# Expert results scattered to token order job by job, and the closing sums shared by VectorE, TensorE and ScalarE

## The chip, the cores and the metric

One core of one Trainium2 chip runs the whole program. The metric is the device time of one execution in microseconds (us), the median over timed runs. A core has TensorE (PE in the profile), VectorE (DVE), ScalarE (ACT), GpSimd (POOL) and SyncE (SP). In this kernel SP and POOL issue all DMAs, each on a queue of its own; the transfers are carried out by the same 16 DMA engines.

## The reference, cut to what matters

```python
x = L0_attn_x                                    # (8, 512, 256) float32
x = _layernorm(x + _L0_attn_ref(x, ...))         # state-space recurrence over 512 steps
x = _layernorm(x + _L0_ffn_ref(x, ...))
x = _layernorm(x + _L1_attn_ref(x, ...))
x = _layernorm(x + _L1_ffn_ref(x, gate_w, fc_w, proj_w))

def _L1_ffn_ref(x, gate_w, fc_w, proj_w):        # E = 8 experts, K = 2 chosen of them
    gates = softmax(xt @ gate_w)                 # 4096 tokens of 256 numbers
    top_v, top_i = top_k(gates, 2);  top_v = top_v / sum(top_v)
    h = gelu(einsum('nd,edf->enf', xt, fc_w))    # 256 -> 1024
    eo = einsum('enf,efd->end', h, proj_w)       # 1024 -> 256
    out = sum over the two chosen experts of top_v * eo
```

The change lies in the last line of the program: the mixture of experts, the sum of a token with its two weighted expert results, and the last layer norm.

## The kernel before, in words

Three phases follow each other. `project_phase` (0 to 296 us) makes the inputs of the recurrence. `stream_phase` (to about 4650 us) runs the recurrence, 2048 updates by GpSimd (L1611) and VectorE (L1649), beside the dense layers, and writes the finished tokens to the DRAM tensor `mixed`. In its half-steps `k`, SP's loop `body` loads `decay` (dt_rows, L713; ScalarE's exponential L1263 waits for it), rows for TensorE, weights, and in every second half-step one piece of 64 rows of a filler into the DRAM tensor `slots` (L799), 512 pieces in all, so that no row of it is ever undefined.

`expert_phase` computes only the chosen experts. Tokens are handled in 8 sequences `s` (groups) of 4 tiles of 128.

- Choosing: for each group TensorE turns x (`turned_x`, L2070) and computes the logits, VectorE picks the two experts (`choose`) and the row in `slots` of each choice (`index`: 4096 rows per expert). GpSimd scatters every tile twice to its rows (L2019, 64 indirect DMAs of 128 rows of 1 KB).
- Jobs: up to `RUN` = 39 jobs, each 256 rows of one expert. For job `j` GpSimd gathers the expert's weights (`fetch(j)`, L1998 and L2002, 1 MB each, double buffered) and the rows of job `j + 2` (`tokens`, L2010, ring `xs` of 4). TensorE's order is turn(j), down(j-1), up(j). ScalarE does the gelu, VectorE copies the result into `made[j % 2]` (`result`, L2341), and SP stores it row by row of the job to `expert_out` (`store`, L1979).
- Close: when the last store has landed, SP raises `all_out`, and GpSimd gathers for each of 32 tiles its two result rows by `slot` (L2036, 64 indirect DMAs of 128 rows of 1 KB into `got`). For each group VectorE adds both results, weighted by `share` (L2356, L2360), takes the statistics (L2364, L2367), waits for ScalarE's 1/sqrt(variance) (Ln L2184, Exp L2186) and normalises (L2371); SP stores the group (L1987).

The order on POOL's queue is written by hand:

```python
            for j in range(2, RUN):
                fetch(j)
                if j + 2 >= XS and j + 2 < RUN:
                    tokens(j + 2)
            pool.wait_ge(slot_ok, 1)
            pool.wait_ge(all_out, 1)
            for c in range(TILES):
                for k in range(2):
                    pool.indirect_dma_start(got[:, k, c], None, d["EXPERT_OUT"], ...
```

## Time and profile before

| | |
|---|---|
| timed runs, median of 3 | 5430.61 us (5424.06 to 5439.41) |
| profiled execution, span of all instructions | 5453.5 us |
| PE / DVE / ACT / POOL busy, share of the span | 86% / 71% / 62% / 73% |
| stretch of the recurrence, 296 to 4320 us | 4024 us |
| stretch of the jobs, 4772 to 5352 us | 580 us |
| from there to the end | 101 us |

For the profiled execution the page gives the span (first to last instruction) and no time measured as in the timed runs; its span lies 22.9 us (0.4%) above their median. Sums below are made inside the span and then applied to the median. A stage is to be read by itself: the engines' shares of the whole span mix a recurrence, a stretch of matmuls and a closing stretch.

### The profile page before, as it was taken

To read this page: it belongs to the slowest core of one execution; us is meant where nothing else is said; L and a number is where in the kernel's file an instruction comes from. 1 tells how busy PE (TensorE), PEld (TensorE's weight loads), DVE (VectorE), ACT (ScalarE), POOL (GpSimd) and SP (SyncE) were. 2 spreads that over 40 slices of the span, in tenths; PEclk is the share of its full clock that TensorE was granted. 3 is DMA by queue.
4 is the path that set the end of the run, shared out by engine and by line. 5 is a ranking of instruction groups with operands and counts; after the bars stand their busy time and mean duration, and the time that the engine had idled before them with its cause. 6 is when DMAs were issued, how large, how long until landed. Compare 5 with 4: busy or idle time off the path is not lost. (4 is left out here: it accounts for less than half of the span.)

```text
span 5453.5 us, 69165 instructions
## 1 busy us (share of the span) xinstructions
PE 4700.0 (86%) x21182; PEld 1804.0 (33%) x21182; DVE 3887.2 (71%) x4378; ACT 3382.7 (62%) x3973; POOL 3994.4 (73%) x2350
## 2 busy tenths in 40 slices
PE   8569999998999899889989998899889887399992
PEld 4301112223223222222222222223222343388882
DVE  6868888888988898789889987988798621400003
ACT  6646666778777877777777777777867633011112
POOL 0079998998999899889989998899899700522224
PEclk9855558989999899899989998999899898599996
DMA  3367676776777677767767776677677521345553
GB/s 114 124 220 256 244 241 236 271 258 236 254 263 261 229 256 254 255 228 256 262 242 252 255 267 236 242 262 263 224 252 262 195 66 43 134 166 175 181 175 113
DMA packets 319255, 1189.13 MB, mean 218 GB/s; under 512 B 77424, under 2 KB 116976, under 8 KB 308912
## 3 DMA queue, kind: packets, MB, share of 16 engines
q1 hardware_dynamic: 296624, 1071.70, 55.8%
q0 software_dynamic: 22272, 113.00, 6.2%
q8 instruction: 182, 2.98, 0.2%
q14 instruction: 177, 1.45, 0.1%
HBM read 1129.21 MB, written 88.87 MB: 223 GB/s over the span
## 5 line engine op out<-in xcount | busy, mean ns | idle before, releaser
L1611 POOL TENSOR_TENSOR s_h<-s_decay,s_h 128x768 f32<-128x768 f32 x2048 | 3705.8, 1849 | 306.4 <-ACT s_decay L1263 283.8
L1649 DVE TENSOR_TENSOR s_h<-s_h,bank 128x1024 f32<-128x1024 f32 x2048 | 2469.8, 1215 | 394.6 <-POOL s_h L1611 210.9
L1263 ACT ACTIVATE s_decay<-s_decay,s_a_neg 128x1536 f32<-128x1536 f32 x1024 | 1606.4, 1569 | 204.1 <-DMA s_decay<-dt_rows 202.8
L895 PE MATMUL bank<-s_h,s_cdiag 128*32 128x512 f32 x8192 | 1259.5, 691 | 10.1 <-ACT s_y L1275 10.1
L1268 ACT ACTIVATE bank<-bank,s_a_neg 128x512 f32<-128x512 f32 x1024 | 672.5, 657 | 678.5 <-PE bank L883 676.0
L869 PE MATMUL bank<-s_vrow,s_brow 9*128 9x512 bf16 x4096 | 847.8, 423 | 277.5 <-DVE s_h L1649 248.5
L869 PEld LDWEIGHTS bank<-s_vrow,s_brow 9*128 9x128 bf16 x4096 | 209.1, 92 | 1504.9 <-issue 1501.6
L1639 DVE TENSOR_TENSOR s_h<-bank,s_h 128x512 f32<-128x512 f32 x1024 | 698.7, 682 | 2.3 <-ACT bank L1268 1.3
L1007 PE MATMUL bank<-m_mb,m_w 128*128 128x512 f32 x1024 | 519.9, 637 | 1.9 <-ACT m_u L1406 1.1
L993 PE MATMUL bank<-m_ma,m_w 128*128 128x512 f32 x1024 | 517.3, 634 | 0.0
L883 PE MATMUL bank<-s_drow,s_unit 3*128 3x512 bf16 x1024 | 433.1, 423 | 76.0 <-DMA s_drow<-dt_parts 46.9
L2172 ACT ACTIVATE e_hid<-bank 128x512 f32<-128x512 f32 x156 | 93.0, 597 | 462.8 <-PE bank L2048 462.8
L895 PEld LDWEIGHTS bank<-s_h,s_cdiag 128*32 128x32 f32 x8192 | 169.7, 114 | 404.5 <-issue 387.0
L2048 PE MATMUL bank<-e_pj,e_hid 128*128 128x256 f32 x1248 | 278.6, 381 | 12.0 <-issue 12.0
L2048 PE MATMUL bank<-e_cT,e_fc 128*128 128x256 f32 x1248 | 277.5, 381 | 0.8 <-DVE e_cT L2336 0.8
L883 PEld LDWEIGHTS bank<-s_drow,s_unit 3*128 3x128 bf16 x1024 | 96.4, 94 | 492.6 <-issue 469.0
L2048 PEld LDWEIGHTS bank<-e_pj,e_hid 128*128 128x128 f32 x1248 | 233.9, 190 | 50.5 <-issue 20.3
L2048 PEld LDWEIGHTS bank<-e_cT,e_fc 128*128 128x128 f32 x1248 | 238.2, 191 | 33.9 <-issue 1.2
L1007 PEld LDWEIGHTS bank<-m_mb,m_w 128*128 128x128 f32 x1024 | 181.6, 195 | 199.9 <-issue 197.7
L993 PEld LDWEIGHTS bank<-m_ma,m_w 128*128 128x128 f32 x1024 | 181.2, 194 | 200.3 <-issue 200.2
L1992 POOL MEMSET e_eps<- 128x1 f32 x1 | 0.1, 99 | 327.2 <-POOLq L2410 327.2
L2336 DVE COPY e_cT<-bank 128x256 f32<-128x256 f32 x39 | 16.6, 425 | 300.4 <-PE bank L2108 300.4
(220 smaller groups left out, 4035.4 us busy)
## 6 DMA issues: line engine op xcount, KB each, us to landing
s_decay<-dt_rows SPq DMA_DIRECT2D x1024, 768.0 KB, 5.4
m_w<-in_units SPq DMA_DIRECT2D x210, 512.0 KB, 5.2
s_vrow<-v_parts SPq DMA_DIRECT2D x1024, 36.0 KB
slots<-in_x_tiles SPq DMA_DIRECT2D x512, 64.0 KB, 4.3
s_brow<-b_parts SPq DMA_DIRECT2D x1024, 9.0 KB
v_parts<-p_part SPq DMA_DIRECT2D x24, 512.0 KB, 3.0
expert_out<-e_made SPq DMA_DIRECT2D x39, 256.0 KB, 6.2
m_w<-w_scaled SPq DMA_DIRECT2D x16, 512.0 KB, 3.7
```

Of the source, the lines that this page charges most:

```text
L869: mm = pe.matmul(bank[:, X0 + n % 2 * PAIR + b], brow[q:q + PAIRS, buf, hf, at * STATE:(at + 1) * STATE], vrow[q:q + PAIRS, buf, hf, at * ...
L883: pe.matmul(bank[:, E0 + hf], unit[q:q + PARTS], drow[q:q + PARTS, buf, t % STEPS], start=True, stop=True).then_inc(e_ps, 1)
L895: mm = pe.matmul(bank[q * 32:(q + 1) * 32, Y0], cdiag[:, hf * LANES + q, at * BLK:(at + 1) * BLK], h[:, t % 2, hf * LANES + q], start=(at ...
L993: mm = pe.matmul(bank[:, j % 4 if tail else M0], w[:, slot, k * P:(k + 1) * P], ma[:, k], start=(k == 0), stop=(k == KH - 1))
L1007: mm = pe.matmul(bank[:, j % 4 if tail else M0], w[:, slot, k * P:(k + 1) * P], mb[:, k], start=(k == 0), stop=(k == KH - 1))
L1263: act.activation(decay[:, k % RING], decay[:, k % RING], ACT.Exp, scale=a_neg[:, 1:2]).then_inc(decay_ok, 1)
L1268: act.activation(bank[:, E0 + k % HALVES], bank[:, E0 + k % HALVES], ACT.Exp, scale=a_neg[:, 1:2]).then_inc(e_ok, 1)
L1611: pool.tensor_tensor(h[:, t % 2, g * PAIR:(g + 1) * PAIR, DCOLS:], decay[:, k % RING, g % 2 * PAIR:(g % 2 + 1) * PAIR], h[:, (t + 1) % 2, ...
L1639: dve.tensor_tensor(h[:, t % 2, hf * LANES:(hf + 1) * LANES, 0:DCOLS], bank[:, E0 + hf].rearrange("p (b d) -> p b d", b=LANES), h[:, (t + ...
L1649: dve.tensor_tensor(h[:, t % 2, g * PAIR:(g + 1) * PAIR], h[:, t % 2, g * PAIR:(g + 1) * PAIR], bank[:, X0 + n % 2 * PAIR:X0 + (n % 2 + 1) ...
L2048: mm = pe.matmul(dst, lhs(k), rhs(k), start=(k == 0), stop=(k == n - 1))
L2172: act.activation(hid[:, r, 2 * m:2 * m + 2].rearrange("p m t -> p (m t)"), bank[:, m], ACT.Gelu).then_inc(up_ok, 1)
```

## The change

Three pieces.

- **Home rows.** A token's row in `slots` grows from 256 to 258 numbers: the two extra ones are `home` (2 × its token number, loaded once) and its second choice (`owner`, VectorE). Job `j` computes on VectorE, from the rows it has gathered, where each result belongs in token order (`goals`: 2 × token, + 1 if the job's expert is the token's second choice; rows that belong to no token go to a dump area). The filler's rows have 258 numbers too.
- **Scatter by job.** GpSimd scatters each job's results to `expert_out` in token order (`give(j - 2)` behind `fetch(j)` and `tokens(j + 2)`, the last three behind the loop). SP's stores and the 64 gathers are gone; at the end SP loads each group's results with one plain DMA of 1 MB (`load`, a ring of `GOT` = 4 buffers).
- **Close.** Of each group's 4 tiles VectorE sums two and TensorE two (identity times x plus two diagonal matrices `weigh` times the results, made by ScalarE in every second job); VectorE takes the statistics of all four and the product `shift` = -mean × rstd; ScalarE normalises (4 activations), into x; SP stores. ScalarE's table for Ln and Exp is set once.

Core of the diff:

```diff
@@ stream_phase, body
-                        sp.dma_start(d["SLOTS_FILL"][(c * HALF_STEPS + k) // FILL_EVERY], d["x_rows"]
+                        sp.dma_start(d["SLOTS_FILL"][(c * HALF_STEPS + k) // FILL_EVERY], d["fill"]
@@ expert_phase
+ROW = DIM + 2
+SUMMED = (0, 1)
+OTHERS = (2, 3)
+GOT = 4
-        x = sb("e_x", [P, TILES, DIM])
-        got = sb("e_got", [P, 2, TILES, DIM])
+        x = sb("e_x", [P, TILES, ROW])
+        got = sb("e_got", [P, GOT, TT, 2, DIM])
+        weigh = sb("e_weigh", [P, BATCH * len(SUMMED), 2, P])
-        xs = sb("e_xs", [P, XS, JT, DIM])
+        xs = sb("e_xs", [P, XS, JT, ROW])
@@ SP
-            for j in range(RUN):
-                store(j, j % 2)
-            sp.wait_ge(made_out, 16 * (RUN + 1))
-            sp.sem_inc(all_out, 1)
+            def load(s):
+                sp.dma_start(got[:, s % GOT], d["EXPERT_OUT_TILES"][s]).then_inc(got_in[s], 16)
+            for r in range(2):
+                sp.wait_ge(made_out[r], 16 * JT * ((RUN + 1 - r) // 2))
+            for s in range(GOT):
+                load(s)
             for s in range(BATCH):
                 sp.wait_ge(y_ok, (s + 1) * TT)
-                sp.dma_start(out[s], got[:, 0, s * TT:(s + 1) * TT]).then_inc(out_dma, 16)
+                if s + GOT < BATCH:
+                    load(s + GOT)
+                sp.dma_start(out[s], x[:, s * TT:(s + 1) * TT, 0:DIM]).then_inc(out_dma, 16)
@@ GpSimd
                 if j >= XS:
                     pool.wait_ge(T_ps, LEAD + j - XS + 1)
+                    pool.wait_ge(goal_ok, j - XS + 1)
+            def give(j):
+                pool.wait_ge(goal_ok, j + 1)
+                pool.wait_ge(made_ok, LEAD + j + 1)
+                for i in range(JT):
+                    pool.indirect_dma_start(d["EXPERT_OUT"], bass.IndirectOffsetOnAxis(ap=goal[:, i, j:j + 1], axis=0),
+                                            made[:, j % 2, i], None).then_inc(made_out[j % 2], 16)
             for s in range(BATCH):
                 pool.wait_ge(x_in[s], 16)
+                pool.wait_ge(home_ok, 1)
+                pool.wait_ge(owner_ok, s + 1)
                 pool.wait_ge(in_ok, s + 1)
@@
-            pool.wait_ge(slot_ok, 1)
-            pool.wait_ge(all_out, 1)
-            for c in range(TILES):
...
+                give(j - 2)
+            for j in (RUN - 2, RUN - 1):
+                give(j)
@@ TensorE
+            def sums(s):
+                n = len(SUMMED)
+                pe.wait_ge(weigh_ok, (s + 1) * 2 * n)
+                if s >= GOT:
+                    pe.wait_ge(y_ok, (s - GOT + 1) * TT)
+                pe.wait_ge(got_in[s], 16)
+                for q, i in enumerate(SUMMED):
+                    dst = bank[:, s % GOT * len(SUMMED) + q, 0:DIM]
+                    pe.matmul(dst, w["ident"][:], x[:, s * TT + i, 0:DIM], start=True, stop=False)
+                    for k in range(2):
+                        mm = pe.matmul(dst, weigh[:, s * n + q, k], got[:, s % GOT, i, k], start=False, stop=(k == 1))
+                    mm.then_inc(sum_ps, 1)
@@ ScalarE
+                if j % 2 == 0 and j // 2 <= BATCH * len(SUMMED):
+                    weights(j // 2 - 1)
             act.wait_ge(eps_ok, 1)
+            act.preload_act_table_set("natural_log_exp_and_others")
...
+                act.wait_ge(ln_ok, s + 1)
+                act.wait_ge(shift_ok, s + 1)
+                for i in range(TT):
+                    c = s * TT + i
+                    whole = bank[:, s % GOT * len(SUMMED) + SUMMED.index(i), 0:DIM] if i in SUMMED else x[:, c, 0:DIM]
+                    act.activation(x[:, c, 0:DIM], whole, ACT.Identity, bias=shift[:, c:c + 1],
+                                   scale=rstd[:, c:c + 1]).then_inc(y_ok, 1)
@@ VectorE
+            def goals(j):
+                dve.wait_ge(xs_in[j % XS], 16 * JT * (j // XS + 1))
+                dve.scalar_tensor_tensor(out=aim[:, :, j], in0=xs[:, j % XS, :, DIM + 1], scalar=whose[:, j:j + 1],
+                                         in1=xs[:, j % XS, :, DIM], op0=ALU.is_equal, op1=ALU.add).then_inc(aim_ok, 1)
...
             def result(j, r):
-                dve.wait_ge(made_free, LEAD + j)
+                if j >= 2:
+                    dve.wait_ge(made_out[r], 16 * JT * (j // 2))
...
+            for s in range(BATCH + 1):
+                if s < BATCH:
+                    dve.wait_ge(got_in[s], 16)
+                    for i in OTHERS:
+                        add(0, s, i)
+                if s:
+                    shifts(s - 1)
+                if s < BATCH:
+                    for i in OTHERS:
+                        add(1, s, i)
+                    statistics(s)
```

How the change moves instructions, at three places (the rows give line, operation, names out<-in and shape; `x2` is a count).

**GpSimd, the end of its queue.** Before, `e_xs` are the gathered tokens, `e_fc` and `e_pj` a job's weights, `e_got` the results gathered at the end:

```order
L2010 DMA e_xs<-slots,e_source 128x256 x2
L1998 DMA e_fc<-in_fc,e_rows 128x2048
L2002 DMA e_pj<-in_pj,e_rows 128x2048
L1998 DMA e_fc<-in_fc,e_rows 128x2048
L2002 DMA e_pj<-in_pj,e_rows 128x2048
L2036 DMA e_got<-expert_out,e_slot 128x256 x64
L1889 UNCONDITIONAL_BRANCH
```

and now, where L2028 is `give` and its last six are the results of jobs 36, 37 and 38:

```order
L2019 DMA e_xs<-slots,e_source 128x258 x2
L2028 DMA expert_out<-e_made,e_goal 18433x256 x2
L2006 DMA e_fc<-in_fc,e_rows 128x2048
L2010 DMA e_pj<-in_pj,e_rows 128x2048
L2028 DMA expert_out<-e_made,e_goal 18433x256 x2
L2006 DMA e_fc<-in_fc,e_rows 128x2048
L2010 DMA e_pj<-in_pj,e_rows 128x2048
L2028 DMA expert_out<-e_made,e_goal 18433x256 x6
L1894 UNCONDITIONAL_BRANCH
```

The 64 gathers are gone from behind the last job; two scatters stand in each job, and two behind the last result.

**SyncE, the expert phase.** Before:

```order
L1968 DMA e_pcol<-in_pcol 128x1
L1970 DMA e_x<-mixed 128x1024 x8
L1973 DMA e_made<-in_pcol 128x1
L1979 DMA expert_out<-e_made 128x2x256 x39
L1987 DMA out<-e_got 128x1024 x8
L1889 UNCONDITIONAL_BRANCH
```

and now, where `e_home` and `e_dump` are two new small tables, and x is written and read in rows of 256 numbers because its rows have 258:

```order
L1979 DMA e_home<-in_home 128x32
L1979 DMA e_dump<-in_dump 128x80
L1981 DMA e_x<-mixed 128x4x256 x8
L1985 DMA e_got<-expert_out 128x2048 x5
L1995 DMA out<-e_x 512x1x256
L1985 DMA e_got<-expert_out 128x2048
L1995 DMA out<-e_x 512x1x256
L1985 DMA e_got<-expert_out 128x2048
L1995 DMA out<-e_x 512x1x256
L1985 DMA e_got<-expert_out 128x2048
L1995 DMA out<-e_x 512x1x256 x5
```

The 39 stores are gone; loads of groups 4 to 7 stand each ahead of a group's store.

**VectorE, one group of the close.** Before, `e_st` and `e_mv` are statistics, the last row is the normalisation:

```order
L2356 SCALAR_TENSOR_TENSOR e_x<-e_got,e_share,e_x 128x256 x4
L2360 SCALAR_TENSOR_TENSOR e_x<-e_got,e_share,e_x 128x256 x4
L2364 BN_STATS e_st<-e_x 128x6 x4
L2367 BN_AGGR e_mv<-e_st 128x2 x4
L2371 TENSOR_SCALAR e_got<-e_x,e_mv,e_rstd 128x256 x4
```

and now, with the previous group's `e_shift` between the two additions:

```order
L2427 SCALAR_TENSOR_TENSOR e_x<-e_got,e_share,e_x 128x256 x2
L2447 SCALAR_TENSOR_TENSOR e_shift<-e_mv,e_rstd 128x4
L2427 SCALAR_TENSOR_TENSOR e_x<-e_got,e_share,e_x 128x256 x2
L2434 BN_STATS e_st<-e_x 128x6 x2
L2437 BN_STATS e_st<-bank 128x6 x2
L2440 BN_AGGR e_mv<-e_st 128x2 x4
```

Half of the additions and the whole normalisation have left VectorE; the statistics of two tiles are read from TensorE's `bank`.

## Rows read from the trace of the kernel before

**Rows 1.** busy time by stage: us, PE, PEld, DVE, ACT, POOL busy (instructions), granted clock, DMA share, GB/s

```profile
296.00:4320.00 4024.00, 3644.82 (x16935) 1036.74 (x16936) 3463.11 (x3546) 2951.25 (x3338) 3703.04 (x2046) 0.89 0.71 251
...
4772.00:5352.00 580.00, 567.09 (x2651) 491.65 (x2652) 42.84 (x77) 105.14 (x196) 137.50 (x145) 1.00 0.51 168
...
5368.00:5454.00 86.00, 0.00 (x0) 0.00 (x0) 50.23 (x160) 24.55 (x32) 56.01 (x55) 0.50 0.42 134
```

**Rows 2.** the end in order of time (start us, us): last job, first and last group

```profile
5352.68 0.69 DVE L2341 COPY e_made<-bank 128x512 f32<-128x512 f32 x1 [14.09 <-PE bank L2048]
5356.42 0.95 POOL L2036 DMA_INDIRECT e_got<-expert_out,e_slot  x1 [32.20 <-SPq L1984]
...
5368.07 1.67 DVE L2356 SCALAR_TENSOR_TENSOR e_x<-e_got,e_share,e_x 128x256 f32<-128x256 f32 x4 [14.70 <-DMA e_got<-expert_out,e_slot]
...
5369.66 1.67 DVE L2360 SCALAR_TENSOR_TENSOR e_x<-e_got,e_share,e_x 128x256 f32<-128x256 f32 x4
...
5371.25 1.40 DVE L2364 BATCH_NORM_STATS2 e_st<-e_x 128x6 f32<-128x256 f32 x4
...
5372.56 0.36 DVE L2367 BATCH_NORM_AGGREGATE e_mv<-e_st 128x2 f32<-128x6 f32 x4
...
5374.61 1.28 ACT L2186 ACT_TABLE_LOAD   x1
...
5376.22 1.38 DVE L2371 TENSOR_SCALAR e_got<-e_x,e_mv,e_rstd 128x256 f32<-128x256 f32 x4 [3.29 <-ACT e_rstd L2186]
...
5439.52 0.95 POOL L2036 DMA_INDIRECT e_got<-expert_out,e_slot  x1 [0.30 <-issue]
5442.24 1.67 DVE L2356 SCALAR_TENSOR_TENSOR e_x<-e_got,e_share,e_x 128x256 f32<-128x256 f32 x4 [1.35 <-DMA e_got<-expert_out,e_slot]
```

**Rows 3.** one job in order of time, all engines

```profile
5079.10 0.38 ACT L2166 ACTIVATE e_cT<-bank 128x256 f32<-128x256 f32 x1
...
5086.28 7.07 PE L2048 MATMUL bank<-e_cT,e_fc 128*128 128x256 f32 x32
...
5086.72 0.95 POOL L2002 DMA_INDIRECT e_pj<-in_pj,e_rows  x1 [6.93 <-PE bank L2048]
...
5089.23 0.96 POOL L2010 DMA_INDIRECT e_xs<-slots,e_source  x1 [0.30 <-issue]
...
5093.63 0.95 POOL L1998 DMA_INDIRECT e_fc<-in_fc,e_rows  x1 [3.43 <-PE bank L2048]
```

**Rows 4.** DMA of the expert stage (4770 to 5353 us): KB each, median us to landing

```profile
expert_out<-e_made SPq DMA_DIRECT2D x38, 256.0 KB, 6.2
```

**Rows 5.** DMA issues of 1 KB rows and of whole groups: KB each, median us to landing

```profile
out<-e_got SPq DMA_DIRECT2D x8, 512.0 KB, 3.0
...
v_parts<-p_part SPq DMA_DIRECT2D x24, 512.0 KB, 3.0
```

**Rows 6.** busy time in a stretch whose DMA engines are full (columns as in Rows 1)

```profile
4759.00:4771.00 12.00, 0.00 (x0) 0.00 (x0) 0.00 (x0) 0.00 (x0) 9.26 (x10) 0.50 0.96 372
```

**Rows 7.** the tile e_fc: duration of its matmuls, ns min/median/max

```profile
L2048 PE MATMUL bank<-e_cT,e_fc x1248: 379/379/763, 4774.0 to 5344.3; 128*128 128x256 f32 x179
```

**Rows 8.** start of the expert phase in order of time

```profile
4657.25 0.43 SPq L1968 DMA_DIRECT2D e_pcol<-in_pcol  x1
4657.73 4.32 SPq L1970 DMA_DIRECT2D e_x<-mixed  x8
...
4661.36 3.75 PE L2070 MATMUL bank<-e_ident,e_x 128*128 128x128 f32 x16 [18.10 <-DMA e_x<-mixed]
...
4675.89 1.07 POOL L2019 DMA_INDIRECT slots<-e_x,e_slot_in  x1 [21.27 <-DVE e_slot_in L2241]
```

**Rows 9.** the tensor slots: duration of the issuing instruction, ns min/median/max, first and last start

```profile
L799 SPq DMA_DIRECT2D slots<-in_x_tiles x512: 495/556/2302, 319.2 to 4314.1; - x171
...
L2019 POOL DMA_INDIRECT slots<-e_x,e_slot_in x64: 965/969/1075, 4675.9 to 4756.2; - x64
```

**Rows 10.** who waited for whom in the recurrence (296 to 4320 us): us, times, longest

```profile
ACT s_decay L1263 <- DMA s_decay<-dt_rows: 202.8, 149, 12.4
```

More of the change, by code:

```diff
@@ L1929, in expert_phase @@
         slotf = sb("e_slotf", [P, 2, TILES])
-        slot = sb("e_slot", [P, 2, TILES], U32)
         whose = sb("e_whose", [P, JOBS])
@@ L1935, in expert_phase @@
         rstd = sb("e_rstd", [P, TILES])
+        shift = sb("e_shift", [P, TILES])
         eps = sb("e_eps", [P, 1])
@@ L2143, in _ @@
             down(RUN - 1, (RUN - 1) % 2, (RUN - 1) // 2)
+            def sums(s):
[10 more added lines that the diff above has]
+                    mm.then_inc(sum_ps, 1)
+            for s in range(BATCH):
+                sums(s)
         @block.scalar
@@ L2173, in gelu, with weights @@
                                    ).then_inc(up_ok, 1)
+            def weights(n):
+                c = n // len(SUMMED) * TT + SUMMED[n % len(SUMMED)]
+                for k in range(2):
+                    act.activation(weigh[:, n, k], w["ident"][:], ACT.Copy, scale=share[:, 2 + k, c:c + 1]
+                                   ).then_inc(weigh_ok, 1)
             turned(0)
             gelu(0, 0)
+            act.wait_ge(share_ok, 4)
             for j in range(1, RUN):
@@ L2252, in _ @@
                     choose(s - 1)
+                    owner(s - 1)
                 if s >= 2:
@@ new lines, in add, with statistics @@
+            def add(k, s, i):
+                c, n = s * TT + i, s * (TT - len(SUMMED)) + OTHERS.index(i) + 1
+                if k:
+                    dve.wait_ge(sum1, n)
+                dve.scalar_tensor_tensor(out=x[:, c, 0:DIM], in0=got[:, s % GOT, i, k], scalar=share[:, 2 + k, c:c + 1],
+                                         in1=x[:, c, 0:DIM], op0=ALU.mult, op1=ALU.add).then_inc(sum2 if k else sum1, 1)
+            def statistics(s):
+                for i in OTHERS:
+                    dve.wait_ge(sum2, s * len(OTHERS) + OTHERS.index(i) + 1)
+                    dve.bn_stats(st[:, s * TT + i], x[:, s * TT + i, 0:DIM]).then_inc(st_ok, 1)
+                for q, i in enumerate(SUMMED):
+                    dve.wait_ge(sum_ps, s * len(SUMMED) + q + 1)
+                    dve.bn_stats(st[:, s * TT + i], bank[:, s % GOT * len(SUMMED) + q, 0:DIM]).then_inc(st_ok, 1)
+                for n, i in enumerate(OTHERS + SUMMED):
+                    dve.wait_ge(st_ok, s * TT + n + 1)
+                    dve.bn_aggr(mv[:, s * TT + i], st[:, s * TT + i]).then_inc(mv_ok, 1)
@@ new lines, in shifts @@
+            def shifts(s):
+                tiles = slice(s * TT, (s + 1) * TT)
+                dve.wait_ge(ln_ok, s + 1)
+                dve.wait_ge(mv_ok, (s + 1) * TT)
+                dve.scalar_tensor_tensor(out=shift[:, tiles], in0=mv[:, tiles, 0], scalar=-1.0, in1=rstd[:, tiles],
+                                         op0=ALU.mult, op1=ALU.mult).then_inc(shift_ok, 1)
+            dve.wait_ge(share_ok, 4)
+            for s in range(BATCH + 1):
[6 more added lines that the diff above has]
+                if s < BATCH:
+                    for i in OTHERS:
+                        add(1, s, i)
+                    statistics(s)
```

113 lines of the change are left out of this document (49 added, 64 removed).

## The prediction

> **What bounds the kernel now.** I read the stages first, because the shares over the whole span mix them. In the recurrence GpSimd is busy 3703 of 4024 us; in the stretch of the jobs TensorE is busy 567 of 580 us at the full clock (2.4 GHz); in the last 86 us TensorE does nothing, and neither VectorE (50 us) nor ScalarE (25 us) nor the DMA engines (42%) is full [rows 1]. A stage in which nothing is full is bound by an order. The timeline of the end shows which one. The last result is copied from 5352.68 us; the first gather starts at 5356.42 and the 64th at 5439.52, so 63 of them take 83.1 us, 1.32 us each; the first group's sums start at 5368.07, the last group's at 5442.24, 2.7 us behind the last gather [rows 2], and 11.3 us on, of which 3.0 are the last store [rows 5], the span ends at 5453.5 us. The close is bound by GpSimd writing one indirect DMA after another, and after each eighth VectorE has its group long before the next. The change is aimed at the 101 us behind the last matmul, so its gain cannot exceed that.
>
> **The close, new.** Step by step, on the clock of the profiled execution:
>
> - Copy of the last result ends at 5353.4. Two scatters are issued by GpSimd, the second from 5353.5 + 1.26 = 5354.8 (1.26 us is the pitch between the start of e_pj and of the second e_xs, 2.51 us for two [rows 3]). An indirect transfer of the same size landed 2.7 us after its start (5439.52 to 5442.24 [rows 2]). So the results lie in DRAM at 5357.5. Upper bound: 6.2 us to landing, as SP's stores take when they queue beside weights [rows 4]; I take 2.7, since no weights are in flight any more.
> - First load. The first x group, 0.52 MB, was used 3.6 us after its issue [rows 8]. Full DMA engines moved 372 GB/s [rows 6], so another 0.52 MB is 1.4 us: 1.05 MB arrives after 5.0 us, at 5362.5. Before, the first group could start at 5368.1.
> - VectorE per group. Additions start 0.40 us apart (four in 1.59, from 5368.07 to 5369.66), statistics 0.33 (four in 1.31), the four aggregations 0.36 [rows 2]. Four additions, four statistics, the aggregations and one shift on 4 numbers a lane (no row; between 0.1 and 0.2 us, as one of the four aggregations at 0.09 and a gap) give 1.59 + 1.31 + 0.36 + 0.2 = 3.5 us. It was 6.3 us of work plus a wait of 3.3 us for ScalarE, in which two table loads of 1.28 us lay [rows 2]; those loads are gone, and the wait is filled with the next group's first additions.
> - TensorE: 6 matmuls per group. Their pace is 7.07 us for 32 = 0.22 us at the full clock [rows 3]; at the clock of 0.50 that the close shows now [rows 1] (1.2 GHz) a matmul takes twice as long (379 against 763 ns at most [rows 7]): 2.7 us per group, below 3.5.
> - ScalarE: Ln and Exp, about 0.7 us without the table loads (3.29 less 2 x 1.28), then 4 activations of 0.38 us at most [rows 3]: 2.3 us per group, below 3.5.
> - DMA: 8.4 MB in and 4.2 MB out are 12.6 MB, at 372 GB/s 33.8 us, 4.2 us per group. That is more than VectorE's 3.5, but the first four loads need not wait for a store. The eighth load has 10.0 MB ahead of it and in it, 26.8 us, behind the 2.2 us of the first load that are not its bytes (3.6 - 1.4): 5357.5 + 2.2 + 26.8 = 5386.5. VectorE would want it at 5362.5 + 7 x 3.5 = 5387.0. The two are level.
> - The end: 5387.0 + 3.5 + 0.7 + 0.2 + 1.4 (four activations, overlapped) = 5392.8, plus 3.0 for the store = 5395.8. Stores now go out of x in rows of 1 KB. The transfer v_parts has such rows and the same 512 KB, and took 3.0 us, like the old store of 4 KB rows [rows 5].
>
> The close is shorter by 5453.5 - 5395.8 = 57.7 us. I take 2 us off for handovers in the eight groups, which is a choice.
>
> "DMA: Bandwidth & Descriptors" of the Trainium skill, section "Where 436 GB/s comes from", says that between HBM and SBUF the HBM side binds at about 358 GB/s for a core. The row has 372 with 4% of the engines' time idle, so the trace does not agree, and it decides; by the page 12.6 MB would take 35.1 us, an estimate, and the sum would be 1.3 us worse.
>
> **The start of the expert phase.** Two more small loads stand ahead of x on SP, 0.47 us each (4657.25 to 4657.73 [rows 8]): 0.95 us. Loads of x in 1 KB rows: 0, by the same v_parts row, up to 0.5. Two `owner` instructions stand ahead of the first slot index on VectorE, 0.1 to 0.2 us each: 0.3. Everything behind is tied to the first scatter at 4675.89 [rows 8] by 64 scatters back to back, 0.97 us each [rows 9] and 1.27 apart, over 81 us; VectorE's 6 new and 6 removed small instructions on job tables hide under them. Together +1.5 us. I take the price of a scatter unchanged at 1032 bytes a row, because e_pj, 8 KB a row, is issued in 0.95 us and a row of 1 KB in 0.96 [rows 3]: the number of rows sets it.
>
> **The jobs.** GpSimd's queue gets two scatters per job, 2.51 us. Today it issues e_pj and two e_xs from 5086.72 to 5090.2 and waits until 5093.63 for TensorE, 3.4 us [rows 3]; 2.5 fit into that, and even late weights would have over a job's length before TensorE needs them, since fetch(j) asks for what up(j) uses one and a half jobs on. `give(j - 2)` waits for a copy that VectorE has done when e_pj is issued, so nothing is held behind it. VectorE may overwrite `made[j % 2]` only when the scatter has landed: issued 5 us behind down(j-2), landed by 6.2 us more at the worst [rows 4], wanted two jobs (29.6 us) behind. VectorE's three tiny goal instructions and ScalarE's two diagonals lie under 7 us of matmuls. DMA is 51% busy there [rows 1], and the bytes are the same. Price 0; if the cover were gone, 39 jobs times what sticks out.
>
> **The recurrence.** The filler moves 64 x 1032 bytes instead of 64 x 1024, 512 times, 0.8% more of 33.5 MB. Of 1010 MB in that stage (251 GB/s for 4024 us [rows 1]) the filler is 3.3%, so 95 us of the DMA engines' busy 2857 us. 0.8% of that is below 1 us. I take 0. Below it nothing is to be had; above, pieces of 4128 bytes no longer start on round addresses, for which there is no row. ScalarE already waits 202.8 us in 149 places for decay rows [rows 10] that queue behind the filler on SP, so what the filler loses counts at those places.
>
> On this the same page of the Trainium skill, section "How a descriptor splits into AXI transactions", says that a piece not starting at a multiple of 256 bytes also pays for the bytes in front of it. By it 4128 bytes would cost at most 6% more than 4096, an estimate: 6 us of engine time spread over the recurrence, 1 to 6 us on the sum if it all showed. No row of this case shows it.
>
> **The sum.** -57.7 + 2 + 1.5 + 0 + 0 = -54 us: 5453.5 becomes 5399 in the span. On the median of the runs, 22.9 us below the span, 5430.6 becomes **5377 us**, 1.0% less.
>
> **The rivals.**
>
> 1. *The close is paced by transfers, not by VectorE.* It now reads and writes at once, and half of its transfers have rows of 1 KB. If stores only reach the 175 GB/s of v_parts taken alone (524 KB in 3.0 us [rows 5]) and loads 372, the bytes take 22.6 + 24 = 46.5 us instead of 33.8: +13, 5390 us. For it: 4.2 against 3.5 us per group is already no margin. Against: the 3.0 us contain a fixed part.
> 2. *The scatters of 1032-byte rows are dearer to issue.* If each row becomes two pieces and the price doubles, 64 x 0.97 = 62 us come back ahead of the first job: 5439 us. It decides from 0.84 us more per scatter. Against: 8 KB and 1 KB rows cost the same.
> 3. *The filler slows the recurrence; the kernel gets slower.* If the odd pieces double its 95 us of engine time and all of it falls on the 149 waits of ScalarE, GpSimd's chain grows by 95 us: 5377 + 95 = 5472 us. It decides from 54 us on the path. For it: DMA is 71% busy there and decay rows do arrive late. Against: 149 of 1024 loads are waited for at all, so a share of the added time, not the whole, would show.
> 4. *GpSimd's longer queue holds up the jobs.* 6 issues of 1.26 us are 7.5 of a job's 14.8 us, so it would take a wait that I have not seen; 1 us per job is 39 us: 5416 us.
>
> **How the numbers follow.** Forecast 0.74, rival 1 0.13, rival 2 0.04, rival 3 in full 0.03, rival 4 0.03, others 0.03. The predicted time is the forecast's. Its own range: downward the handovers and the start may cost nothing (3.5 us), the first load may come 1 us earlier, and two medians of runs that lie 6.5 us under and 8.8 over it may differ by 10 more: 5362. Upward the filler may cost 6, the landing of the last scatter 3.5 and the runs' spread 8.8: 5395. With rival 1, the filler and the spread the upper end is 5405; what is left out is under 2 in 10. 0.3% of this kernel, 16 us, is about what a measurement can tell from no change. Faster by more: forecast, rival 1 and part of the others, 0.91. Within: rivals 2 and 4, 0.05. Slower: rival 3 and what is unforeseen, 0.04.
>
> **What would show it.** Right: the first group's additions start some 6 us earlier after the last matmul than now; groups follow each other at 3.5 to 4.5 us on VectorE; from the last matmul to the end 43 to 46 us instead of 101; jobs still 14.8 us apart and e_fc issued at the same moment after up(j-2); scatters still 1.27 us apart; the recurrence within 5 us of 4024 and ScalarE's wait for decay near 203 us. Wrong: groups at over 5 us with VectorE waiting for e_got (rival 1), a scatter over 1.1 us (2), a wait for decay that has grown by tens of us (3), a TensorE that waits for weights (4).

## The result and the profile after

The change is faster: 5388.73 us median of 4 runs (5380.9 to 5396.29) against 5429.31 us of 4 runs of the kernel before, ratio 0.9917 [0.9899, 0.9935]. That is 40.6 us, with an interval of 35 to 55 us; forecast were 54 us and a time of 5377 in a range from 5362 to 5405. The profiled execution has a span of 5387.5 us. One run of this study (of a_combo, 5703.85 us) went at a granted TensorE clock of 0.766 in place of 0.88 to 0.89 and stands in no ratio or median.

Most of the spread between executions comes from the recurrence: over the 14 profiles of this study it takes 3974 to 4010 us from the first to the last update of `s_h` on GpSimd, and kernels with and without the change lie mixed in that range. So I judge by a stretch that does not contain it. From the load of `e_gate` to the end (the expert phase) it is 4654.51 to 5453.5 = 799.0 us before and 4636.26 to 5387.5 = 751.2 us after: **47.8 us less**. Its parts (here and below such stretches are differences of starts, good to 0.1 us):

| stretch | forecast | before | after | difference |
|---|---|---|---|---|
| `e_gate` load to first scatter (start) | +1.5 | 21.4 | 26.3 | +4.9 |
| first scatter to first `turn` | 0 | 96.2 | 96.4 | +0.2 |
| from there to the copy of the last result | 0 | 580.6 | 581.5 | +0.9 |
| copy of the last result to the end (close) | -57.7 + 2 | 100.8 | 47.0 | -53.8 |

The stages of the kernel after (columns as in [rows 1]); the third row is the close, which answers to the last of [rows 1]:

```profile
296.00:4302.00 4006.00, 3634.43 (x16942) 1035.00 (x16944) 3441.67 (x3546) 2954.72 (x3339) 3706.83 (x2047) 0.89 0.72 252
4754.00:5334.00 580.00, 562.18 (x2624) 487.30 (x2625) 57.12 (x194) 115.47 (x229) 218.42 (x225) 0.99 0.50 172
...
5347.00:5387.00 40.00, 24.81 (x96) 19.86 (x96) 26.82 (x104) 20.01 (x48) 0.00 (x0) 0.84 0.82 312
```

Where GpSimd issued gathers for 83 us with everything else half idle, VectorE is now busy 27 of 40 us and the DMA engines 82% of the time. The recurrence moves about as many bytes (252 GB/s for 4006 us against 251 for 4024) at a DMA share of 0.72 against 0.71.

The close of the kernel after in order of time (start, us), which answers to [rows 2]:

```profile
5340.47 0.69 DVE L2408 COPY e_made<-bank 128x512 f32<-128x512 f32 x1 [14.03 <-PE bank L2063]
...
5343.19 0.96 POOL L2028 DMA_INDIRECT expert_out<-e_made,e_goal  x1 [0.31 <-issue]
...
5345.63 14.58 SPq L1985 DMA_DIRECT2D e_got<-expert_out  x5
...
5350.68 1.67 DVE L2427 SCALAR_TENSOR_TENSOR e_x<-e_got,e_share,e_x 128x256 f32<-128x256 f32 x4 [9.52 <-DMA e_got<-expert_out]
5352.27 0.75 DVE L2434 BATCH_NORM_STATS2 e_st<-e_x 128x6 f32<-128x256 f32 x2
5353.66 0.43 DVE L2437 BATCH_NORM_STATS2 e_st<-bank 128x6 f32<-128x256 f32 x1 [0.65 <-PE bank L2171]
5356.22 0.43 DVE L2437 BATCH_NORM_STATS2 e_st<-bank 128x6 f32<-128x256 f32 x1 [2.13 <-PE bank L2171]
...
5356.85 0.85 DVE L2427 SCALAR_TENSOR_TENSOR e_x<-e_got,e_share,e_x 128x256 f32<-128x256 f32 x2
...
5377.30 0.88 DVE L2427 SCALAR_TENSOR_TENSOR e_x<-e_got,e_share,e_x 128x256 f32<-128x256 f32 x2
```

The first sums start 10.2 us behind the copy (15.4 before), as forecast (9.8). The second group starts 6.2 us on, at 5356.85, because VectorE waits twice for TensorE. The third to the sixth start at 5360.08, 5363.31, 5366.54 and 5369.78, 3.23 us apart; the last two steps are 3.7 and 3.8 us, and the eighth group starts at 5377.30.

TensorE in the first group, and the tile `e_got` over the whole close:

```profile
5350.72 1.19 PE L2169 MATMUL bank<-e_x,e_ident 128*128 128x256 f32 x2 [10.36 <-DMA e_got<-expert_out]
5351.71 1.91 PE L2171 MATMUL bank<-e_got,e_weigh 128*128 128x256 f32 x4
...
5357.58 0.59 PE L2169 MATMUL bank<-e_x,e_ident 128*128 128x256 f32 x2
```

```profile
who waited for it (us, times):
  PE bank L2169: 15.1, 5
  DVE e_x L2427: 9.5, 1
  DVE e_st L2437: 3.2, 4
...
DMA to landing us min/median/max: 5.0/7.1/11.1
```

The same two pieces (the trace shows each matmul of these sums as two pieces) take 1.19 us in the first group and 0.59 later. The granted clock, the number behind the five engines in these rows (columns as in [rows 1]), is 0.50 at first and 1.00 afterwards, 1.2 and 2.4 GHz:

```profile
5350.00:5354.00 4.00, 3.28 (x8) 2.68 (x9) 2.67 (x7) 0.00 (x0) 0.00 (x0) 0.50 1.01 426
...
5358.00:5362.00 4.00, 4.00 (x20) 3.51 (x19) 4.00 (x16) 3.27 (x8) 0.00 (x0) 1.00 0.27 37
```

TensorE had stood for 10.4 us. Of its 15.1 us of waiting for `e_got` 10.4 are that first one; the rest are the loads of the last four groups, which are issued only when a group before has been finished.

One job on GpSimd, which answers to [rows 3]:

```profile
5074.48 0.96 POOL L2010 DMA_INDIRECT e_pj<-in_pj,e_rows  x1 [6.89 <-PE bank L2063]
...
5078.28 1.00 POOL L2028 DMA_INDIRECT expert_out<-e_made,e_goal  x1 [0.30 <-issue]
5079.58 0.98 POOL L2028 DMA_INDIRECT expert_out<-e_made,e_goal  x1 [0.30 <-issue]
5081.38 0.99 POOL L2006 DMA_INDIRECT e_fc<-in_fc,e_rows  x1 [0.82 <-PE bank L2063]
```

The two scatters fill the gap, the wait before `e_fc` is 0.82 us where it was 3.43, and the next job's `e_fc` still follows after 14.78 us. The cover held, with 0.8 us to spare.

The start of the expert phase, which answers to [rows 8]:

```profile
4640.43 8.38 SPq L1981 DMA_DIRECT2D e_x<-mixed  x8
...
4644.40 1.94 PE L2085 MATMUL bank<-e_ident,e_x 128*128 128x128 f32 x8 [19.39 <-DMA e_x<-mixed]
4647.06 1.97 PE L2085 MATMUL bank<-e_ident,e_x 128*128 128x128 f32 x8 [0.71 <-DMA e_x<-mixed]
4648.82 3.42 PE L2063 MATMUL bank<-e_gate,e_cT 128*128 128x8 f32 x16
```

and the 10 us behind the first x in the kernel after, and below it in the kernel before (columns as in [rows 1]):

```profile
4644.40:4654.40 10.00, 9.28 (x44) 8.89 (x44) 3.10 (x21) 1.74 (x4) 0.00 (x0) 0.50 1.01 324
```

```profile
4661.40:4671.40 10.00, 10.00 (x62) 9.65 (x63) 5.31 (x33) 2.03 (x5) 0.00 (x0) 0.67 0.86 338
```

From first x to first scatter it is 18.2 us (14.5 before). TensorE is busy in both, but gets 44 instructions done instead of 62: before, its clock went to 1.00 for a while.

### The profile page after: what moved, and what is told of

Read it like the earlier page. It is cut to its first block and busy times, and to the rows that moved or that the text cites. A ratio compares the mean times of both kernels' runs of the same rounds, so it can differ in the third digit from the quotient of the medians.

```text
span 5387.5 us, 69474 instructions
## 1 busy us (share of the span) xinstructions
PE 4718.6 (88%) x21278; PEld 1827.4 (34%) x21278; DVE 3855.4 (72%) x4448; ACT 3391.4 (63%) x4022; POOL 4011.9 (74%) x2364
## 5 line engine op out<-in xcount | busy, mean ns | idle before, releaser
L1264 ACT ACTIVATE s_decay<-s_decay,s_a_neg 128x1536 f32<-128x1536 f32 x1024 | 1606.5, 1569 | 231.3 <-DMA s_decay<-dt_rows 229.8
L884 PEld LDWEIGHTS bank<-s_drow,s_unit 3*128 3x128 bf16 x1024 | 96.4, 94 | 493.6 <-issue 471.1
```

What stands on the lines that cost most here:

```text
L884: pe.matmul(bank[:, E0 + hf], unit[q:q + PARTS], drow[q:q + PARTS, buf, t % STEPS], start=True, stop=True).then_inc(e_ps, 1)
L1264: act.activation(decay[:, k % RING], decay[:, k % RING], ACT.Exp, scale=a_neg[:, 1:2]).then_inc(decay_ok, 1)
```

## The experiments

The time of each kernel is beside runs of the kernel before on the same chip; where the times can't decide, stretches of the trace do.

**Does the filler in odd pieces, or x in 1 KB rows, cost anything?** The kernel before with one part of the change each, the change with round filler pieces, and the change again as the control.

b_fill (before, filler pieces of 64 x 1032 bytes):

```diff
-                        sp.dma_start(d["SLOTS_FILL"][(c * HALF_STEPS + k) // FILL_EVERY], d["x_rows"]
+                        sp.dma_start(d["SLOTS_FILL"][(c * HALF_STEPS + k) // FILL_EVERY], d["fill"]
...
-        d["SLOTS_FILL"] = slots.rearrange("(n r) d -> n r d", n=CHUNKS * HALF_STEPS // FILL_EVERY)
+        d["SLOTS_FILL"] = flat.rearrange("(n r d) -> n r d", n=CHUNKS * HALF_STEPS // FILL_EVERY, d=DIM + 2)
```

b_x258 (before, x in rows of 258 numbers, whose last two nobody uses):

```diff
-        x = sb("e_x", [P, TILES, DIM])
+        x = sb("e_x", [P, TILES, DIM + 2])
-                sp.dma_start(x[:, s * TT:(s + 1) * TT], d["MIXED"][s]).then_inc(x_in[s], 16)
+                sp.dma_start(x[:, s * TT:(s + 1) * TT, 0:DIM], d["MIXED"][s]).then_inc(x_in[s], 16)
...
```

a_fill4096 (after, the same `slots` filled by 512 pieces of 64 x 1024 bytes and 4 more in the first chunk):

```diff
-        d["SLOTS_FILL"] = slots.rearrange("(n r) d -> n r d", n=CHUNKS * HALF_STEPS // FILL_EVERY)
+        d["SLOTS_FILL"] = flat[0:EXPERTS * REGION * DIM].rearrange("(n r d) -> n r d", n=CHUNKS * HALF_STEPS // FILL_EVERY, d=DIM)
+        d["SLOTS_REST"] = flat[EXPERTS * REGION * DIM:].rearrange("(n r d) -> n r d", n=4, d=DIM)
...
```

after_again is the change without an edit.

> The kernel before with one edit: the 512 filler pieces have 16 x 4128 bytes, as in the change, instead of 16 x 4096 (the slots tensor is 0.8% longer, nothing else differs). Theory A (the filler costs what the change lost beyond the expert phase): the median gain of 40.6 us is 7.2 us less than the 47.8 us by which the expert phase of the trace is shorter, so this kernel should be about 7 us slower than the kernel before, and ScalarE's wait for decay rows should rise from 202.8 us towards the 229.8 us of the changed kernel. Theory B (the 7 us are spread between runs): within 3 us of before, and the wait for decay differs from 202.8 by as much in any other run.

> The kernel before with one edit: the rows of x in SBUF are 258 numbers apart, so x is loaded in rows of 1 KB instead of 4 KB, and nothing else (no more small loads, no owner, scatters of 1024 bytes). Theory A (the loads in 1 KB rows delay the second group, and through the gap TensorE stays at its lower clock): SP's issue of the eight loads takes 8.4 us instead of 4.3, the granted clock in the first 11 us of TensorE's work is 0.50 instead of about 0.7, and the first scatter is 3 to 4 us later after the first load's issue (before 18.2, changed kernel 22.1). Theory B (the owner instructions and the two small loads make the 4.9 us): first scatter within 0.5 us of 18.2. The total should be 3 to 4 us longer by A, 0 by B.

> The changed kernel with one edit: the filler in 516 pieces of 16 x 4096 bytes instead of 512 of 16 x 4128. Theory A (odd pieces cost about 7 us): 7 us faster than the changed kernel run beside it. Theory B: within 3 us of it.

> The changed kernel again, as a control beside the three others on the same chip. Expected 0.990 to 0.993 of before, 38 to 55 us less; its trace shows how far the recurrence and the wait for decay vary between two executions of one program (by theory that the first trace's recurrence, 19 us shorter than before's, is spread: the recurrence here differs from it by up to 20 us).

| kernel | median, runs | ratio to before | recurrence | `e_gate` to first scatter | close | expert phase |
|---|---|---|---|---|---|---|
| b_fill | 5438.04, 12 | 1.0002 [0.9984, 1.0019] | 3974.1 | 21.3 | 100.3 | 798.7 |
| b_x258 | 5440.19, 12 | 1.0009 [0.9995, 1.0023] | 3985.1 | 21.4 | 101.7 | 801.7 |
| a_fill4096 | 5384.95, 6 | 0.9899 [0.9876, 0.9923] | 4003.5 | 25.5 | 45.8 | 749.6 |
| after_again | 5390.42, 6 | 0.9913 [0.9889, 0.9937] | 3997.8 | 25.4 | 46.2 | 749.9 |

The odd pieces cost nothing that shows. With them ScalarE waits 195.0 us for decay rows in b_fill, 198.3 in after_again and 229.8 in the first profile of the change; without them 202.8 before [rows 10], 206.0 in b_x258 and 222.2 in a_fill4096. The wait moves by 30 us between two executions of one program, so it decides nothing. a_fill4096 ran 5.5 us below after_again, between the 7 us of theory A and the 3 of theory B; the intervals of the two overlap, and its recurrence was 5.7 us longer, not shorter. A cost of a few us is not excluded. The narrower loads of x make SP issue for 8.3 us instead of 4.3 and bring the first x 0.4 us later (7.26 us behind `e_gate` against 6.85), but the first scatter comes after 21.4 us as before. Its expected low clock did not come either (1.00 for some us, as before). So the start's 4.9 us are not theirs, and the control shows most of them again (+4.0). The expert phase of b_x258 is 2.7 us longer than before, all of it behind the first scatter; its cause was not looked for. The change is worth 47 us in the control's runs; the profiled phases say 49.

**What bound the close: the gathers, or the sums?** The kernel before with the new sums alone, and with the gathers alone replaced (8 plain loads of 1 MB; this leaves out the placing of results in token order).

b_newclose takes `sums`, `weights`, `add`, `statistics`, `shifts` and ScalarE's four activations from the change and keeps the 64 gathers (against the change):

```diff
-                pe.wait_ge(got_in[s], 16)
+                pe.wait_ge(got_in[s], 16 * 2 * TT)
...
-                        mm = pe.matmul(dst, weigh[:, s * n + q, k], got[:, s % GOT, i, k], start=False, stop=(k == 1))
+                        mm = pe.matmul(dst, weigh[:, s * n + q, k], got[:, k, s * TT + i], start=False, stop=(k == 1))
...
```

b_plain (against the kernel before):

```diff
-            for c in range(TILES):
-                for k in range(2):
-                    pool.indirect_dma_start(got[:, k, c], None, d["EXPERT_OUT"],
...
+            for s in range(BATCH):
+                sp.dma_start(got[:, s], d["OUT_GROUPS"][s]).then_inc(got_in[s], 16)
...
```

> The kernel before, with the 64 gathers kept at the end but the sums, the statistics and the normalising of the change (two tiles of a group on TensorE, ScalarE normalises, its table set once). Theory A (the close before is bound by GpSimd writing the gathers): the 64 gathers still take 83 us, so only what stands behind the last gather becomes shorter; from the copy of the last result to the end 96 to 99 us in place of 100.8, the whole 2 to 5 us less. Theory B (the engines' sums were a bound of their own): the close falls by tens of us, towards 60.

> The kernel before with its stores by SP and its old sums on VectorE, the 64 gathers replaced by 8 plain loads of 1 MB in the order of the jobs (it leaves out the placing of the results in token order). Theory A (with the gathers gone, the old work of a group is the next bound: 6.3 us on VectorE and 3.3 us of waiting for ScalarE and its two table loads): 8 groups 9.5 us apart, the close 85 to 92 us in place of 100.8, so removing the gathers alone brings 9 to 16 us of the change's 54. Theory B (the gathers were the whole of it): the close is near the 47 us of the change, or within 10 us of that.

b_newclose: 5436.76 us (7 runs), ratio 1.0014 [0.9996, 1.0032], close 97.9 us. By the profile the new sums alone bring 2.9 us; the times show no gain (2 us less to 17 us more). VectorE waits for the gathers before each group, and the last group comes 2.8 us behind the 64th gather as before:

```profile
5420.88 0.95 POOL L2041 DMA_INDIRECT e_got<-expert_out,e_slot  x1 [0.30 <-issue]
...
5423.67 0.88 DVE L2396 SCALAR_TENSOR_TENSOR e_x<-e_got,e_share,e_x 128x256 f32<-128x256 f32 x2 [4.91 <-DMA e_got<-expert_out,e_slot]
```

b_plain: 5415.15 us (10 runs), ratio 0.9966 [0.9950, 0.9982], 10 to 27 us less by the times, close 77.7 us. Removing the gathers alone brings 23.1 us by the profile. I had expected 9 to 16, because I took 3.3 us of waiting for ScalarE in every group; from the second group on it is 1.95 and the groups are 8.09 us apart:

```profile
5365.37 0.36 DVE L2362 BATCH_NORM_AGGREGATE e_mv<-e_st 128x2 f32<-128x6 f32 x4
5367.68 1.38 DVE L2366 TENSOR_SCALAR e_got<-e_x,e_mv,e_rstd 128x256 f32<-128x256 f32 x4 [1.95 <-ACT e_rstd L2181]
5368.97 1.67 DVE L2351 SCALAR_TENSOR_TENSOR e_x<-e_got,e_share,e_x 128x256 f32<-128x256 f32 x4
```

2.9 and 23.1 us alone, 53.8 together. The close had two bounds one behind the other: 10.5 us a group on GpSimd's queue, and behind it 8.1 us on the chain VectorE, ScalarE, VectorE. Neither part is worth much without the other.

**Is the new close paced by VectorE or by transfers (rival 1)?**

a_onlyV:

```diff
-SUMMED = (0, 1)
-OTHERS = (2, 3)
+SUMMED = ()
+OTHERS = (0, 1, 2, 3)
...
```

a_got8 (the sums still go round 8 banks):

```diff
-GOT = 4
+GOT = 8
...
-                    dst = bank[:, s % GOT * len(SUMMED) + q, 0:DIM]
+                    dst = bank[:, s % 4 * len(SUMMED) + q, 0:DIM]
...
```

> The changed kernel with all four tiles of a group summed by VectorE (TensorE does no sums, ScalarE still normalises). Theory A (the close is paced by VectorE): four more additions of 0.40 us a group, less the wait for TensorE in the first group; groups 4.8 us apart in place of 3.2 to 3.7, close 53 to 57 us in place of 46 to 47. Theory B (my rival 1, the close is paced by transfers at over 4.2 us a group): groups stay under 4.4 us apart and the close is longer by 4 us or less.

> The changed kernel with room for all eight groups of results, so that no load waits for a store (the loads of groups 4 to 7 are issued at once behind the first four). Theory A (in the last three groups VectorE and TensorE wait for loads issued late, 3.7 us apart against 3.2): the groups stay 3.2 us apart to the end, the close gets 1 to 2 us shorter, 44 to 45.5 us, with the stores then being what ends it. Theory B (the bytes are the limit, whatever the order): stores fall behind the loads, the close is as long as before or up to 2 us longer.

a_onlyV: 5397.46 us (4 runs), ratio 0.9949 [0.9932, 0.9965], close 55.1 us. Groups are 4.81 us apart and VectorE never stops (columns as in [rows 1]):

```profile
5340.00:5374.00 34.00, 0.00 (x0) 0.00 (x0) 34.00 (x121) 17.10 (x41) 0.00 (x0) 0.50 0.82 267
```

Four more additions a group lengthen the close by 8 to 9 us, so VectorE paces it and rival 1 falls. a_got8: 5390.20 us (4 runs), ratio 0.9924 [0.9902, 0.9947], close 45.4 us, with all groups behind the first 3.23 us apart to the end. The late loads were worth 1.1 us between groups. The closes of the change spread (47.0, 46.2, 45.8; a_startwarm and a_late below, whose close is the same code, have 46.8 and 45.9) for another reason: the step from the first to the second group is 6.0 to 6.2 us in after and a_startwarm and 4.9 to 5.1 in the other three. The granted clock goes with it: in the third and fourth us behind the first sums it is 0.50 in the two, and 0.71 to 0.77 in the three. In a_got8 the step is 6.2 us, too. Without it the five closes take 40.8 to 41.1 us and a_got8 39.2, so the larger ring is worth some 1.6 us in the profile.

**Is TensorE's clock what is late, in the first group of the close and at the start?**

a_warm:

```diff
+            for q in range(48):
+                pe.matmul(bank[:, 7, 0:DIM], w["ident"][:], fc[:, 0, 0:DIM], start=True, stop=True)
             for s in range(BATCH):
                 sums(s)
```

a_startwarm:

```diff
             pe.wait_ge(w_in, 16 * NW)
+            for q in range(12):
+                pe.matmul(bank[:, 7, 0:P], w["ident"][:], w["before"][:], start=True, stop=True)
```

a_late (VectorE copies `home` ahead of its first `owner`):

```diff
             for k in names:
-                sp.dma_start(w[k][:], d[k]).then_inc(w_in, 16)
+                if k not in ("home", "dump"):
+                    sp.dma_start(w[k][:], d[k]).then_inc(w_in, 16)
...
+                if s == 1:
+                    for k in ("home", "dump"):
+                        sp.dma_start(w[k][:], d[k]).then_inc(late_in, 16)
```

> The changed kernel with 48 matmuls of 256 columns, whose result nobody reads, between the last job and the first sums, where TensorE otherwise does nothing for 10 us. Theory A (the first group of the close is slow because TensorE's clock has fallen to 0.50 while it waited): the granted clock stays at 1.00 until the sums start, VectorE's wait of 0.65 + 2.13 us for TensorE in the first group goes, and the close gets 2 to 3 us shorter, 43.5 to 44.5 us. Theory B (the first sums are late for their data, not for the clock): the wait and the close stay as they are, 46 to 47 us. The jobs and the start are as in the change either way.

> The changed kernel with 12 matmuls of 128 columns, whose result nobody reads, on TensorE between the arrival of the small tables and the arrival of the first group of x (the change leaves it idle there for 19.4 us, the kernel before for 18.1 us). Theory A (the start is 3 us late because TensorE's clock stays at 0.50 through the first groups, where before it rose to 1.00 for some 6 us): the clock rises within the first two groups as before, and from the first load of x to the first scatter 18 to 19 us in place of 21.2 to 22.2. Theory B (the loads of x in pieces of 1 KB or the new small instructions are what is late): the clock may rise, the stretch stays above 20.5 us.

> The changed kernel with the two added small tables loaded behind the second group of x, no longer ahead of the first. The loads themselves are worth 0.95 us from the load of e_gate to the first scatter. Theory A (they also move TensorE's first work so that its clock stays at 0.50): 25.4 to 26.3 us becomes 21.5 to 22.5, with the clock at 1.00 for some microseconds in the first groups as in the kernel before. Theory B (the clock stays low for another reason, or is not what is late): 24.4 to 25.4 us, only the 0.95 less.

a_warm: 5390.77 us (4 runs), ratio 0.9917 [0.9901, 0.9934], close 54.7 us: neither theory's number, by my own mistake. The 48 matmuls are 96 pieces in the trace and ran 10 us too long:

```profile
5340.02 20.88 PE L2175 MATMUL bank<-e_fc,e_ident 128*128 128x256 f32 x96
5360.74 0.59 PE L2169 MATMUL bank<-e_x,e_ident 128*128 128x256 f32 x2
5361.18 1.03 PE L2171 MATMUL bank<-e_got,e_weigh 128*128 128x256 f32 x4
```

It still shows part of the point: behind them the first sums take 0.59 and 1.03 us, not 1.19 and 1.91. And it shows an error in the prediction (below).

a_startwarm: 5384.28 us (4 runs), ratio 0.9899 [0.9881, 0.9918]. The clock goes to 1.00 just as the first x is turned, and from first x to first scatter it is 13.2 us (18.2 in the change, 14.5 before). The 12 matmuls, 24 pieces in 4.82 us, and a small load (`e_ones`) that took 1.14 us to issue instead of 0.43 held the first x up until 11.1 us behind `e_gate` (8.1 in the change), so of the 5 us only 1 to 2 are left: first scatter after 24.3 us. From the first load of x it is 19.4 us, just above the 18 to 19 of theory A and below theory B's 20.5. The 13.2 us are not the clock's alone: the later groups of x had more time to arrive.

a_late: 5378.97 us (4 runs), ratio 0.9905 [0.9888, 0.9922]. First scatter after 25.6 us, clock 0.50 throughout: moving the tables does not bring the clock back, as theory B has it, though 25.6 lies just outside its 24.4 to 25.4. The 0.95 us don't show, because in this execution one small load (`e_before`) took 1.53 us to issue instead of 0.43.

The profiles of all kernels together speak for the clock. Where it rose near the first x, first x to first scatter took 13.2 to 15.1 us (eight profiles); where it stayed at 0.50, 17.2 to 18.3 us (six). It rose in all five profiles of before and its variants, in none of six of the change, after_again, a_fill4096, a_onlyV, a_got8 and a_late, in the two with unread matmuls at the start, and in a_warm, whose start is the code of the change and whose x came later still, behind a load of `e_before` that took 1.72 us to issue (TensorE idle 20.7 us, against 19.4 to 19.6 in the six and 18.1 to 18.5 in the five). So neither the length of the idle time alone nor the code of the start decides it. Only the change has two profiles of one kernel (0.50 in both), so it is not known whether a kernel always falls on the same side; what decides it **stays open**. That the clock makes the 3 us is argued from this split and from TensorE being busy all along, and not shown by a run that changes the clock alone.

**Does a version with all of it beat both?** The edits of a_late and a_got8, and those of a_startwarm and a_warm with other counts:

```diff
-            for q in range(12):
+            for q in range(5):
...
-            for q in range(48):
+            for q in range(22):
```

> The changed kernel with what the runs so far suggest put together: the two added tables loaded behind the second group of x; 5 unread matmuls of 128 columns before the first group of x; room for all eight groups of results; 22 unread matmuls of 256 columns before the first sums (44 pieces of 0.22 us, 9.7 us, where 48 of them took 20.9 us and held the sums up). Theory A (the start and the first group of the close are late for TensorE's clock, the last three groups for loads issued late): from the load of e_gate to the first scatter 21.5 to 23 us, the close 42.5 to 43.5 us, the expert phase 743 to 745 us in place of 750 to 751; the time some 7 us below that of the change, which the spread of the runs can just about hide. Theory B (these waits only trade places with others): the expert phase stays at 748 us or more.

First scatter after 22.5 us, close 42.8 us, expert phase **743.3 us** in place of 751.2 and 749.9: all three in the ranges of theory A. VectorE's waits in the first group are 0.24 us in all, in place of 0.65 + 2.13:

```profile
5345.30 9.66 PE L2182 MATMUL bank<-e_fc,e_ident 128*128 128x256 f32 x44
5355.72 0.67 PE L2176 MATMUL bank<-e_x,e_ident 128*128 128x256 f32 x2 [0.76 <-DMA e_got<-expert_out]
```

```profile
5358.58 0.43 DVE L2448 BATCH_NORM_STATS2 e_st<-bank 128x6 f32<-128x256 f32 x1 [0.24 <-PE bank L2178]
```

The times can't show these 7 us: 5390.28 us median of 5 runs (5359.64 to 5411.67), ratio 0.9905 [0.9871, 0.9939], beside 0.9917 and 0.9913 of the change. By its profile it beats both; by its time it beats only the kernel before.

## Why the prediction was right, point by point

- **What bounds the close.** Right, and shown: new sums with the gathers kept, 2.9 us; and with only the gathers replaced the old chain becomes the bound, 8.1 us a group.
- **The close, -57.7 + 2.** Measured -53.8. The first load was forecast 9.8 us behind the copy and its sums started after 10.2. VectorE per group: forecast 3.5 us, measured 3.23; four aggregations and the shift cost 0.36 us on the engine's clock, where I had put 0.56. The seven steps from the first to the eighth group were forecast at 24.5 us and took 26.6: the first step 6.2, the last two 3.7 and 3.8. From there to the end 8.8 were forecast and 10.2 measured; ScalarE's activation takes 0.55 us (two in 1.02 to 1.09), not "0.38 us at most".
- **The step that failed: TensorE in the close.** "6 matmuls per group ... 7.07 us for 32 = 0.22 us" read the pitch of a piece as that of a matmul. One fp32 matmul of the program is two pieces in the trace (48 are x96, 12 are x24), so a group costs 12 x 0.22 = 2.6 us at the full clock and 5.3 at half (as long as the first group took, 5350.72 to 5355.98), above VectorE's 3.5 and not "2.7 us per group, below 3.5". By my own assumption of a clock of 0.50 throughout, TensorE would have paced the close. It was luck that a second error undid the first: the clock did not stay at 0.50 once the sums ran. What is left of both is the 2.8 us that VectorE waits in the first group. On this the Trainium skill ("TensorE: Matmul & The Clock Gate", section "Why this matters for your kernels") advises against idle gaps between bursts of matmuls; the trace agrees (10.4 us of standing, then 1.19 us for what later takes 0.59), and in a_combo, which filled the gap, the first step between groups is 3.54 us in place of 4.9 to 6.2 in the profiles of the change.
- **DMA, "4.2 us per group ... the two are level".** Wrong in size: engines full of plain loads moved more than the 372 GB/s of [rows 6], which are GpSimd's indirect loads. In a_combo (4 us windows, columns as in [rows 1]):

```profile
5357.60:5361.60 4.00, 4.00 (x20) 3.52 (x19) 3.76 (x16) 1.88 (x5) 0.00 (x0) 1.00 1.02 430
5361.60:5365.60 4.00, 4.00 (x20) 3.50 (x19) 4.00 (x18) 3.13 (x8) 0.00 (x0) 1.00 1.01 422
```

  At 425 GB/s 12.6 MB would be 29.6 us, 3.7 a group. The next two windows of a_combo (5369.6 to 5377.6), in which the loads end and the stores of 1 KB rows follow, have 329 and 381. Since the first store starts only with the third group (5360.25), most loads lie ahead of the stores and are not what is waited for, except the last ones, which a ring of four issues late. The 358 GB/s that the prediction quoted from the Trainium skill ("DMA: Bandwidth & Descriptors") is farther off still. The Trainium skill's page "Perfetto Trace Analysis", section "Roofline", says that a core whose neighbour is idle can pull more than that share, up to some 435 GB/s; the rows agree, with 422 to 430.
- **The start, +1.5.** Measured +4.9, and +4.0 in the control. The two small loads are there (0.95, x loads start 4.17 us behind `e_gate` instead of 3.22), the narrow loads cost 0.4 where I took "0, up to 0.5", and `owner` costs 0.08 us on VectorE's clock, not 0.3. The step that failed here is the sum "Together +1.5 us", which takes TensorE's work between the first x and the first scatter as unchanged: 3.6 of the 4.9 us (2.7 of the 4.0 in the control) were added between first x and first scatter, where TensorE stayed at the clock of 0.50, and they were absent in each profile in which the clock rose.
- **The jobs, 0.** Right to 1.1 us of 678, for the reason given (the 1.1 us are not the scatters': b_x258, which has none in its jobs, shows 1.8, and a_warm, which has them, 0.4); the wait left over is 0.82 us, where 3.43 - 2.51 = 0.92 was the sum.
- **The recurrence, 0.** Right: 1.0002 [0.9984, 1.0019] with 12 runs. What the Trainium skill ("DMA: Bandwidth & Descriptors", section "How a descriptor splits into AXI transactions") says of pieces at unaligned starts, by the prediction's estimate 1 to 6 us on the sum, can be neither seen nor excluded: the interval reaches 8 to 10 us to either side.
- **Price of a scatter, unchanged.** 965/969/1059 ns after, 965/969/1075 before [rows 9], with 1032 bytes a row; in the jobs 0.97 to 1.00. The rows show that a row's length does not set the price; that their number does is not shown, since all have 128.
- **The rivals.** 1 (transfers pace): a_onlyV and the 3.23 us speak against it. 2 (dearer scatters), 3 (filler) and 4 (GpSimd's queue) did not happen, by the three points above.

The sum was forecast at -54.2 and is -47.8 by the profile: of the missing 6.4 us the start has 3.4, the close 1.9 and the stretch between them 1.1. The median's other 7 us are within its interval.

## What to carry to other kernels

When a stage is bound by an order of issues, look at once for the bound behind it, and price both: here removing the gathers alone was worth 23 us, the cheaper sums alone 3, and both together 54. Before multiplying the time between two pieces of a trace by a count, check on a known instruction how many pieces the trace shows for one operation of the program. Where TensorE stands idle before a short burst, cost the burst at both clocks that the rows show, the one after standing and the full one; filling the gap with work that nobody reads is a cheap test, if it is sized in pieces.

## What the runs showed of the hardware that was not expected

- TensorE's granted clock behind the first x: 1.00 for some microseconds or 0.50 for all of the start, with the same matmuls waiting. Some 3 us go with it, and kernels that differ only in what comes 700 us later fall on different sides (after_again 17.2 us from first x to first scatter, a_warm 15.1).
- Plain loads of 8 KB a partition from DRAM moved 422 to 430 GB/s over four windows of 4 us in a_combo, also where the last of them overlap with sums on three engines. Loads of x in 1 KB pieces moved 325 to 375 in windows of 2 and 4 us with full engines (the change and its variants, b_x258), in the 4 KB pieces of the kernel before 408 to 418 (three windows of 2 us, 4663.4 to 4669.4).
- In four profiles one of the small loads ahead of x took longer to issue than 0.43 us: `e_before` in a_warm (1.72) and a_late (1.53), `e_ones` in a_startwarm (1.14) and a_combo (1.39). These four kernels ran on one chip, eight of the ten others on two other chips, and in the ten none of these loads was slow. No cause shows in the profile, and whether the chip or the code of these kernels makes it is not shown.
